# A graph layer with the message product applied before the gathers: B folded into the stored rows, no turn and product at a quad's end, counts by 200 columns, and a sort with fewer small steps

## The reference

```python
h_self = x @ W_lin + b_lin
messages = x[col] @ W_msg + b_msg
msg_sum = segment_sum(messages, row)
counts = segment_sum(1, row)
h_agg = msg_sum / max(counts, 1)
h = relu(concat([h_self, h_agg]) @ W_upd + b_upd)
out = layernorm(x + h)            # mean and variance over the 128 features, no weights
```

## Time and profile before

| | |
|---|---|
| time, median of 3 runs (lowest, highest) | 1358.66 us (1356.97, 1359.03) |
| profiled execution: its own time, its span | 1359.65 us, 1357.9 us |
| busy: PE, DVE, ACT, POOL | 1203.5, 996.9, 681.1, 633.6 us |
| chain that ended last, by engine | PE 63%, DVE 28%, issue 4%, ACT 2%, DMA 1%, POOL 1% |
| chain, largest lines | L1268 29%, L1282 20%, L1293 6%, L805 6%, L783 5% |
| granted TensorE clock, mean | 0.939 |

### The profile page before, as it was taken

The page is one execution under the profiler, slowest core; times in us unless marked ns, Lnnn a source line. Parts: engine busy times, 40 slices in busy tenths (PEclk is TensorE's granted clock), DMA queues, the critical chain, the costliest instruction groups (busy, mean ns, idle before and its releaser), DMA issues.

```text
span 1357.9 us, 42359 instructions
## 1 busy us (share of the span) xinstructions
PE 1203.5 (89%) x16556; PEld 742.2 (55%) x16556; DVE 996.9 (73%) x2602; ACT 681.1 (50%) x978; POOL 633.6 (47%) x673
## 2 busy tenths in 40 slices
PE   3869779689886399999999999999999999999996
PEld 2869678689885144444444444444444444444443
DVE  7999899999995556666666666666666666666665
ACT  1323323111101267666666666666666666666663
POOL 2000000000000477767777777777777777767772
PEclk9979779678786699999999999999999999999998
DMA  7333333243000545555554555455555555555531
GB/s 108 103 102 114 97 96 107 72 111 97 6 1 6 185 136 155 156 153 158 153 150 130 154 149 145 138 152 154 153 158 155 156 156 156 156 154 158 156 89 41
DMA packets 124987, 168.87 MB, mean 124 GB/s; under 512 B 34771, under 2 KB 93952, under 8 KB 124716
## 3 DMA queue, kind: packets, MB, share of 16 engines
q1 hardware_dynamic: 92226, 101.17, 23.1%
q0 software_dynamic: 31280, 64.23, 19.8%
q10 hardware_dynamic: 1290, 0.78, 0.3%
HBM read 142.91 MB, written 23.21 MB: 122 GB/s over the span
## 4 chain that ended last, share of the span: by engine, by line
PE 63%; DVE 28%; issue 4%; ACT 2%; DMA 1%; POOL 1%; DVEq 0%; SPq 0%; POOLq 0%; ACTq 0%
PE slot L1268 29%; PE acc L1282 20%; PE acc L1293 6%; DVE big L805 6%; DVE big L783 5%; PE slot L1318 2%; DVE big L835 2%; DVE big L842 2%; ACT big L573 2%; DVE big L841 2%; PE acc L1301 1%; PE acc L1159 1%; DVE big L1009 1%; PE slot L1309 1%; DVE big L790 1%
## 5 line engine op out<-in xcount | busy, mean ns | idle before, releaser
L573 ACT ACTIVATE big<-slot 128x768 bf16<-128x768 f32 x750 | 567.5, 809 | 311.3 <-PE slot L1268 311.3
L646 POOL DMA_INDIRECT big<-x,dst_at x500 | 481.4, 963 | 192.4 <-issue 73.3
L1268 PE MATMUL slot<-big 128*128 128x384 bf16 x2300 | 445.5, 328 | 32.8 <-ACT big L573 16.7
L950 DVE TENSOR_SCALAR big<-big,iota_k 128x512 bf16<-128x512 f16 x575 | 196.5, 371 | 281.3 <-PE slot L1268 267.8
L1268 PEld LDWEIGHTS slot<-big 128*128 128x128 bf16 x2300 | 189.9, 97 | 262.1 <-issue 137.8
L1282 PE MATMUL acc<-big 32*128 32x385 bf16 x6000 | 309.3, 324 | 0.0
L1282 PEld LDWEIGHTS acc<-big 32*128 32x128 bf16 x6000 | 124.0, 93 | 160.7 <-issue 110.6
L641 POOL MEMSET big<- 128x4 bf16 x6 | 0.3, 96 | 443.0 <-issue 443.0
L650 POOL DMA_INDIRECT big<-x,sp_i x150 | 144.9, 966 | 65.9 <-PE slot L1268 34.4
L960 DVE TENSOR_TENSOR big<-col_lo,iota_lo 128x512 bf16<-128x512 f16 x375 | 156.2, 417 | 0.0
L1159 PE MATMUL acc<-big,tri 125*125 125x100 f16 x1600 | 120.1, 241 | 8.2 <-DVE big L783 7.8
(11 more groups left out here) (148 smaller groups left out, 943.0 us busy)
## 6 DMA issues: line engine op xcount, KB each, us to landing
big<-rows SPq DMA_DIRECT2D x25, 1920.0 KB
x<-big SPq DMA_DIRECT2D x19, 480.0 KB, 3.1
big<-x,dst_at POOLq DMA_INDIRECT x500
big<-x SPq DMA_DIRECT2D x32, 192.0 KB, 2.4
big<-in_x SPq DMA_DIRECT2D x24, 256.0 KB
big<-base SPq DMA_DIRECT2D x24, 256.0 KB
out<-big SPq DMA_DIRECT2D x24, 256.0 KB, 5.4
big<-in_x SPq DMA_DIRECT2D x19, 320.0 KB, 4.5
```

The source lines that it names most:

```text
L573: act.activation(xg[n % NX][:, :, 0:F3], slot[z % 2][:, :, 0:F3], ACT.Copy).then_inc(s["xg_ready"], 1)
L646: pool.indirect_dma_start(out=xg_d[:, c, 0:F3], out_offset=None, in_=x3_dram, in_offset=bass.IndirectOffsetOnAxis(ap=dst_at[:, q, c:c + 1] ...
L950: last = nc.vector.tensor_scalar(W[R_ % NW_][:, k, :].rearrange("p (c h n) -> p c h n", c=4, h=4), brow[q % NB].rearrange("p (h c n) -> p ...
L1268: ins = nc.tensor.matmul(slot[z % 2][:, j, 0:F3], W[R_ % NW_][:, k, (c % 4) * P:(c % 4 + 1) * P], xwin[:, win_at(c) + k, :], start=k == 0, ...
```

## The change

1. **B by blocks.** x is taken in XB = 25 blocks of 512 columns. A block's turned copy is multiplied by B and by A in one go. What is split into three bf16 parts and stored as rows is x @ B, read from PSUM, instead of x. `turn_x` runs one step ahead, and `make_base` stands ahead of `add_ranks` on PE.
2. **A quad's end.** The sums are then already those of x @ B. `turn`, its copy on ACT, `update`, and the division of the sums go; `layer` takes sum times 1/count plus base in one instruction for each of the four groups, at r = 7 (root at 8, norm at 9). The slots alternate strictly.
3. **Counts.** One matmul counts a pair for both chunks, 200 columns instead of 100; `dupc` is added by one more matmul within `add_ranks`.
4. **Shorter route.** Without the add of `dupc`, and with both values (lo and dst) scaled by 512 and made by one instruction, six small instructions behind the reduction, seven with the add, become four.
5. **prepare** is called for 20 chunks and then, at u = 3, for the other 60 at once. `decode` works on both values together, in 7 instructions instead of 10.
6. **Before the branch.** The largest rank is taken before the last `decode` instead of behind it, and SP loads the first two `brow` before it waits for the flag.

```diff
-    XB, XJ = 20, 5
+    XB, XJ = 25, 4
-        TURN, UPDATE, ROOT, LAYER, NORM = 5, 8, 10, 9, 11
+        LAYER, ROOT, NORM = 7, 8, 9
-            work += 1024 * (r == TURN) + 2048 * (r == UPDATE)
...
+            sp.wait_ge(s["T_made"], U)
+            sp.wait_ge(s["rows_stored"], 16 * NS)
+            load_brow(0)
+            load_brow(1)
+
             sp.wait_ge(s["flag_known"], 1)
...
             def split_1(b):
                 dve.wait_ge(s["hi_cast"], b + 1)
-                dve.wait_ge(s["x_turned"], b + 1)
+                if b > 0:
+                    dve.wait_ge(s["lo_made"], b)
                 n = xb_rows(b)
-                x3b = x_blk[b % 2][0:n, :].rearrange("p (j f) -> p j f", f=F)
-                nc.vector.tensor_tensor(x3b, x3b, x3_blk[b % 2][0:n, :, 0:F], ALU.subtract).then_inc(s["r1_made"], 1)
+                nc.vector.tensor_tensor(r1_blk[0:n, :].rearrange("p (j f) -> p j f", f=F), slot[1][0:n, 1, :].rearrange("p (j f) -> p j f", f=F),
+                                        x3_blk[b % 2][0:n, :, 0:F], ALU.subtract).then_inc(s["r1_made"], 1)
...
-                k = mark(nc.vector.tensor_tensor(k2, r2, two_chunks(dupc, u), ALU.add))
-                after(k)
...
                 k0 = mark(nc.vector.tensor_scalar(col(s32), k2, SL - 0.5, -float(SL), ALU.is_gt, ALU.mult))
-                k1 = mark(nc.vector.tensor_scalar(col(sa), k2, SL - 0.5, 255.0, ALU.is_gt, ALU.mult))
-                k3 = mark(nc.vector.tensor_scalar(col(sbb), k2, SL - 0.5, 511.0 / 512.0, ALU.is_gt, ALU.mult))
+                k1 = mark(nc.vector.tensor_scalar(col(sbb), k2, SL - 0.5, 511.0 / 512.0, ALU.is_gt, ALU.mult))
                 after(k0)
                 k0 = mark(nc.vector.tensor_tensor(col(s16), k2, col(s32), ALU.add))
                 after(k1)
-                k1 = mark(nc.vector.scalar_tensor_tensor(out=col(vlo), in0=col(sa), scalar=1.0, in1=two_chunks(lo1, u), op0=ALU.add, op1=ALU.mult))
-                after(k3)
-                k3 = mark(nc.vector.scalar_tensor_tensor(out=col(vdst), in0=col(sbb), scalar=1.0 / 512.0, in1=two_chunks(dst1, u), op0=ALU.add, op1=ALU.mult))
+                k1 = mark(nc.vector.scalar_tensor_tensor(out=val[0:EP, :, :], in0=sbb[0:EP, :].unsqueeze(1).to_broadcast([EP, 2, 2 * T]), scalar=1.0 / 512.0,
+                                                         in1=nodes[0:EP, u, :, :], op0=ALU.add, op1=ALU.mult))
...
-            prepare(0)
+            prepare(0, CS)
...
                 if u == 3:
-                    prepare(1)
-                if u == 12:
-                    prepare(2)
-                if u == 20:
-                    prepare(3)
+                    prepare(CS, C)
...
                 def layer(q):
-                    dve.wait_ge(s["h_made"], q + 1)
...
-                    nc.vector.tensor_tensor(Y, base4[q % 2], slot[z % 2][:, 0, :].rearrange("p (h f) -> p h f", f=F), ALU.add).then_inc(s["h_read"], 1)
-                    dve.wait_ge(s["h_read"], q + 1)
+                    for h in range(4):
+                        ins = nc.vector.scalar_tensor_tensor(out=Y[:, h, :], in0=S[:, h, :], scalar=cnt[:, 1, h:h + 1], in1=base4[q % 2][:, h, :], op0=ALU.mult, op1=ALU.add)
+                    ins.then_inc(s["S_read"], 1)
+                    dve.wait_ge(s["S_read"], q + 1)
...
-                for k in range(2):
-                    for a in range(TP):
-                        for j in range(2):
-                            ins = nc.tensor.matmul(R_ps[u % 2][:, k * H:(k + 1) * H], tri16[0:EP, 0:EP], OH[u % 4][0:EP, k * TP + a, :, j],
-                                                   start=a + j == 0, stop=a + j == TP)
+                of = OH[u % 4][0:EP, :, :, :].rearrange("p (k a) h j -> p k a h j", k=2)
+                for a in range(TP):
+                    for j in range(2):
+                        ins = nc.tensor.matmul(R_ps[u % 2].rearrange("p (k h) -> p k h", k=2), tri16[0:EP, 0:EP], of[:, :, a, :, j],
+                                               start=a + j == 0, stop=a + j == TP)
...
+                for k, w in ((1, B), (0, A)):
+                    for j in range(XJ):
+                        ins = nc.tensor.matmul(slot[1][0:n, k, j * F:(j + 1) * F], xT_blk[:, j * P:j * P + n], w, start=True, stop=True)
```

More of the change, by code:

```diff
@@ L107, in gnn_program @@
         dst_rows = pre.take(EC, i32)[0:C, :]
-        m7 = shaped(pre.take(CS * T, i32), "p (c t) -> p c t", t=T)
+        m7 = shaped(pre.take((C - CS) * T, i32), "p (c t) -> p c t", t=T)
+        same = [shaped(pre.take((C - CS) * T, f16), "p (c t) -> p c t", t=T) for _ in range(3)]
         x_blk = [pre.take(XJ * F, f32) for _ in range(2)]
@@ L111, in gnn_program @@
         xT_blk = pre.take(XJ * P, f32)
+        r1_blk = pre.take(XJ * F, f32)
         base_blk = [pre.take(XJ * F, f32) for _ in range(2)]
@@ L306, in xb_rows, with two_chunks @@
             return (P if b < XB - 1 else XRP)
+        def two_chunks(a, u):
+            return a[0:EP, 2 * u:2 * u + 2, :].rearrange("p c (a j) -> p (c a) j", j=2)
         def bc(a, n):
             return a.unsqueeze(2).to_broadcast([a.shape[0], a.shape[1], n])
[L312 to L321, removed]
         block = ctx.enter_context(nc.Block())
@@ L525, in take_xT @@
                     act.wait_ge(s["base_made"], b)
[L526 removed]
+                act.activation(xT_blk, slot[0][:, 0, :], ACT.Copy).then_inc(s["xT_taken"], 1)
             def take_base(b):
@@ L812, in route @@
                 dve.wait_ge(s["Q_added"], u + 1)
-                r2 = red[0:EP, :].rearrange("p (a j) -> p a j", j=2)
-                with nc.allow_low_precision("whole numbers below 2501 in fp16; 64 and over are told apart"):
-                    nc.vector.tensor_reduce(r2, Q_ps[b].rearrange("p (a h j) -> p a j h", h=NH, j=2), AX.X, ALU.add).then_inc(s["ranks_taken"], 1)
+                k2 = two_chunks(r_all, u)
+                with nc.allow_low_precision("whole numbers below 2521 in fp16; 64 and over are told apart"):
+                    nc.vector.tensor_reduce(k2, Q_ps[b].rearrange("p (a h j) -> p a j h", h=NH, j=2), AX.X, ALU.add).then_inc(s["ranks_taken"], 1)
                 dve.wait_ge(s["ranks_taken"], u + 1)
-                k2 = r_all[0:EP, 2 * u:2 * u + 2, :].rearrange("p c (a j) -> p (c a) j", j=2)
-                k = mark(nc.vector.tensor_tensor(k2, r2, two_chunks(dupc, u), ALU.add))
-                after(k)
                 def col(a):
@@ L1062, in general @@
                 made[0] = before_branch
+                for k in range(NB):
+                    dve.wait_ge(brow_loaded[k], 16)
                 dve.wait_ge(s["T_made"], U)
```

228 lines of the change are left out of this document (91 added, 137 removed).

## The result

The kernel before took 1358.85 us (median of 4 runs, 1356.97 to 1360.19) and the changed one 1396.47 us (4 runs, 1394.11 to 1397.61): a ratio of 1.0273, 95% interval 1.0261 to 1.0285. I had forecast 1287 us. All later runs were made in five sets, each beside runs of the kernel before; in two of the five it took 1358 to 1360 us, in the other three 1509 to 1529 us, for a reason that lies outside the kernel, so a time is read against the kernel before of its own set.

A forecast was written before the change was run, and what follows sets the result against it. TensorE was taken to bound the quads, VectorE the sort. Quads -46.8, last quad's end -2.5, sort -14.3, rank -1.8, `brow` wait -10.2, first quad +4.1 make -71.5 us: median 1287, eight in ten 1271 to 1305.

The forecast's parts named there:

- `layer` at r = 7: Quad's end: moving layer earlier costs nothing, as it ends over a microsecond before ScalarE reaches the root.
- turn and product: Quads, on TensorE: dropping both rows saves 1.95 us a quad, 46.8 us over 24 quads.
- What is next in line is POOL: Quads: 26 gathers take about 32.8 us against 33.2, leaving 0.4 us of slack a quad, where it had 2.4.
- Gathers bound the quads: Rival, chance 0.15: GpSimd's pace makes it wait, another 1 us a quad, 1311 us, between 1300 and 1330.
- "Slower" by the clock: Rival, chance 0.02: TensorE's waits for late gathers lower its clock in every quad, 4 us each, 1387 us.
- The other half of "slower": Rival, chance 0.01: all gathers take the longest 1.243 us, making a quad 40.1 us and the time 1459.
- The sort: Stage before the quads: shorter steps, `prepare`, splits, stalls and half clock sum to -14.3 us.
- One-hot behind reduction: Sort steps on VectorE: 1.17 us from reduction to one-hot becomes 0.82, 40 times, -13.6 us.
- The long `prepare`: Sort: one call for 60 chunks takes 18.4 us in place of 25.4, -7 us; a fixed-charge estimate gave 5.
- The +3 for VectorE's wait in `split_1`: Sort: the second `decode` falls into a step with a block, so a half-clock wait recurs, about +3 us.
- The first quad: Start of the quads: gathers lose their lead of ten microseconds over TensorE, +4.1 us, bounds +1 and +9.
- The last quad's end: Behind the last reduction: product wait and division go, the 0.69 us sum becomes 1.14, -2.5 us.

The follow-up runs named there:

- norm at 11: The changed kernel with only layer, root and norm put back to r = 9, 10, 11: 1295.37 us, ratio 0.9522 to the kernel before.
- burst at step 28: The changed kernel, SyncE holding x, base, output and `brow` loads until step 28 (30 half-run steps a quad) is gathered: 1306.48 us, ratio 0.9631.
- three microseconds of hold: The changed kernel, SyncE holding its burst of transfers until step 24 of the quad is gathered: 1396.66 us, ratio 1.0257 to the kernel before.

## Why the prediction was wrong

**The quads: the step that failed.** "`layer` at r = 7 ends more than a microsecond before ScalarE reaches the root at r = 8 [...] so I cost that move at nothing." I followed the moved steps to ScalarE only. The norm moved as well, from r = 11 to r = 9, and SyncE's queue stands behind it with four transfers. This was the term that had to be priced: not +0 but, with what it set off, 24 x (37.76 - 33.45) = 103 us. The sign that I had set for failure, quads over 34 us apart, came true. With the burst where it had been, the step's own figure holds: 33.45 us against 33.2, and turn and product were worth 1.7 us a quad where I had 1.95.

**"What is next in line is POOL".** The sum of 26 gathers against a quad's length, 0.4 us of slack, was the wrong account. What decides is the lead of each gather at its own place: with norm at 11 pairs 8 and 9 are used 5.6 and 5.0 us behind their second gather. One that TensorE waited for with `brow` out of the way was there after 2.7 to 3.0 us (pair 9 with the burst at step 28), one issued beside `brow` mostly after 7 to 9. So some 2 us of delay are hidden, and the rest is not.

**The rivals.** "Gathers bound the quads" had the right engine and the right wait, and 1 us a quad for what came to 4.3; it had GpSimd's pace as the mechanism, not a transfer beside it. "Slower" by the clock, to which I gave 0.02, named 1387 us and a limit of 2.9 us a quad. The waits, 3.2 us a quad, do bring the lower clock after them, for the three groups of the timeline above, not for 8 us; the other 1.1 of the 4.3 are what is left for the clock (in the windows above TensorE is busy 34.17 us with `brow` and 32.34 without, for the same matmuls). Its own cause, late gathers, had been left without a price. The other half of "slower", gathers that get slow on GpSimd, came true for two gathers a quad, 0.45 and 0.8 us each, and cost nothing in the quad without `brow`.

**The sort.** Forecast with the rank and the branch -26.3 us to the first window, measured -30.9. One-hot behind reduction: 0.86 us (399.38 - 398.52), forecast 0.82. The long `prepare` made its step 20.1 us longer, forecast 18.4; that saves 5.3 us where the rows gave 7, and near the 5 of the prediction's second estimate by a fixed charge for each instruction. The +3 for VectorE's wait in `split_1` did not come, and the old one of 4.11 us went too: L776 waited 0.9 us in all. Those 7 us are more than the whole difference of 4.6. The first window comes 1.38 us behind the flag, with no wait for `brow`: right.

**The first quad**: +8.8 against +4.1; one wait of 6.3 us for a gather lies in it, and that gather, at 457.72, was issued 0.09 us ahead of a `brow` load: the same collision, in a quad that I had priced by GpSimd's lead alone. That the delay isn't carried on, norm at 11 shows, which leaves the first quad as it is.

**The last quad's end**: -2.5 us, as forecast.

## What to carry to other kernels

When a step moves, follow its semaphore to every queue that waits for it, and most of all to a queue of transfers: the step may cost nothing where it lands, and still fire megabytes into a stretch in which small gathers are due. Compare for each gather its issue, its use, and the nearest large transfer, and put the large one behind the last gather that is needed soon; a wait that holds it by a few microseconds is free if its data is only needed a stage later. When a cure does nothing, look first whether the wait has moved to the next user: here three microseconds of hold were one pair too short, and nearly eight were enough. And look in a trace for the quad that lacks a suspect: the last ones, here without `brow`, had the answer before any experiment.

## What the runs showed of the hardware

**Gathers in a burst.** A pair whose second gather went out beside `brow` was mostly used after 7 to 9 us, with TensorE waiting for it; clear of it, pairs that TensorE waited for came after 2.7 to 3.0 us (pair 9, burst at step 28). The spill gathers say the same: they land after 6.4 us in the median of the whole changed kernel, and in its last two quads, without `brow`, so (the view of line L631 from 1318 us on):

```profile
DMA to landing us min/median/max: 3.5/3.6/3.9
```

`brow` itself takes 11.1 to 12.8 us from issue to landing in the quads. What it takes with nothing beside it no run shows: the two `brow` loads ahead of the quads, half a microsecond apart, took 9.4 and 14.1 us. The Trainium skill (DMA: Bandwidth & Descriptors, Queues, rings and completion order) says that each DMA engine takes turns between its queues, a packet at a time. That agrees with a gather that is slowed but not put behind the whole burst; no run here shows the turns themselves.

**Gathers lengthened on GpSimd.** In the changed kernel, with norm at 9, gathers 19 and 21 of 20 of the 25 quads take 1.40 and 1.75 us in place of 0.95, whether the burst lies at 19.6 or at 22.7 us, and with norm at 11 they don't; so it is VectorE's order, not the transfers. The Trainium skill (SBUF — State Buffer, SBUF: two separate sides) says that GpSimd can't write descriptors while VectorE runs in a two-port mode. The long gathers in the timeline above lie across window instructions of VectorE (L922 at 651.30 and 652.71), which agrees; that these and no others hold it up was not isolated, and the norm's four instructions (L1000 at 650.26) lie across a gather that keeps its 0.95 us.

**A condition in which quads take 42 us.** In three of five sets the kernel before took 1509 to 1529 us. It isn't the chip alone: two of the three ran on the chip that the record numbers 11, and so did one of the sets with 1358 to 1360 us. The sort is unchanged there; the quads are not. With norm at 11 the same two page rows read, first in that condition, then in the other:

```profile
L564 ACT ACTIVATE big<-slot 128x768 bf16<-128x768 f32 x750 | 567.9, 809 | 490.3 <-PE slot L1240 464.7
L1240 PE MATMUL slot<-big 128*128 128x384 bf16 x2300 | 470.2, 327 | 178.5 <-ACT big L564 135.1
```

```profile
L564 ACT ACTIVATE big<-slot 128x768 bf16<-128x768 f32 x750 | 567.6, 809 | 283.8 <-PE slot L1240 283.7
L1240 PE MATMUL slot<-big 128*128 128x384 bf16 x2300 | 443.2, 329 | 18.9 <-ACT big L564 16.5
```

The instructions are as long as ever, but TensorE waits eight times as long for ScalarE, and ScalarE 1.6 times as long for TensorE. In the timeline of that condition ScalarE starts 1.04 us behind the end of the matmuls that it waits for:

```profile
717.68 0.48 PE L1240 MATMUL slot<-big 128*128 128x384 bf16 x2
...
719.20 1.51 ACT L564 ACTIVATE big<-slot 128x768 bf16<-128x768 f32 x2 [1.48 <-PE slot L1240]
...
719.39 0.95 POOL L631 DMA_INDIRECT big<-x,sp_i  x1 [0.99 <-remote]
```

ScalarE sits idle for 1.48 us here, and for 1.5 to 1.8 before most of its copies; in the other condition it is most often 0.67. Some of GpSimd's waits are put down to "remote" there (51 waits, 41 us), as the last row, and none in the other condition. What delays them I don't know. Quads of 42 us give every gather several microseconds more; TensorE hardly waits for a pair there (with the burst at step 28 it is idle ahead of the pairs' matmuls for 0.9 us in all), and the changed kernel's variants are all some 2% faster than the kernel before, so the collision can't be seen. The changed kernel itself was not timed in it.
